# A four-layer graph network on one core: two neighbour sums of the kernel split over the column halves of TensorE

## The reference, cut to what matters

```python
# layer 2: three attention convolutions; the first has 64 inputs, 4 heads of 128 channels
h = (x @ W).reshape(n, heads, ch)
e = leaky_relu(alpha_src[src] + alpha_dst[dst], 0.2)
ex = exp(e - m[dst]);  den = segment_sum(ex, dst)
out = segment_sum(h[src] * (ex / den[dst]), dst)      # mean over heads, + bias
# layer 3: mean over neighbours
neigh_sum = segment_sum(features[src], dst)
degree = clip(segment_sum(ones, dst), 1.0)
combined = concatenate([features, neigh_sum / degree], -1) @ W + b
```

## Time and profile before

| What | Value |
|---|---|
| median of three runs | 5350.39 us |
| the profiled execution | 5350.4 us, span 5348.6 us |
| PE busy | 4615.0 us, 86% of the span |
| DVE busy | 3798.2 us, 71% |
| ACT busy | 1823.8 us, 34% |
| POOL busy | 1990.0 us, 37% |

### The profile page before, as it was taken

The page is one execution under the profiler, slowest core; times in us unless marked ns, Lnnn a source line. Parts: engine busy times, 40 slices in busy tenths (PEclk is TensorE's granted clock), DMA queues, the critical chain, the costliest instruction groups (busy, mean ns, idle before and its releaser), DMA issues.

```text
span 5348.6 us, 118073 instructions
## 1 busy us (share of the span) xinstructions
PE 4615.0 (86%) x41659; PEld 3580.5 (67%) x41660; DVE 3798.2 (71%) x5768; ACT 1823.8 (34%) x3064; POOL 1990.0 (37%) x1717
## 2 busy tenths in 40 slices
PE   6999999888886969999579999588886888888886
PEld 3998888888885555555479999564544555555554
DVE  6988888877771057777466666455114999999998
ACT  0000000000001527777337777336341333333332
POOL 3888888882002057100000000000004766666663
PEclk6999999999996879999789999789777999999998
DMA  1000000000000000000000000000001111111113
GB/s 51 6 6 5 5 5 5 5 5 1 0 0 2 0 10 10 4 2 2 20 3 4 4 4 4 17 2 11 1 3 39 37 36 36 36 36 36 36 37 25
DMA packets 203918, 74.19 MB, mean 14 GB/s; under 512 B 169275, under 2 KB 189578, under 8 KB 203658
## 3 DMA queue, kind: packets, MB, share of 16 engines
q0 software_dynamic: 52448, 31.60, 3.5%
q1 hardware_dynamic: 151338, 40.69, 3.5%
HBM read 57.25 MB, written 14.88 MB: 13 GB/s over the span
## 4 chain that ended last, share of the span: by engine, by line
PE 63%; DVE 23%; issue 8%; DVEq 3%; DMA 2%; ACT 1%; POOL 0%; SPq 0%; ACTq 0%; POOLq 0%
PE ps L1182 62%; DVE adj L1140 8%; DVE adj L1132 5%; DVE scratch L851 5%; DVEq L849 1%; DVEq L336 1%; DVE adj L1145 1%; DMA r_dram<-adj 0%; DMA hwork<-gat_out_a 0%; DMA hwork<-gat_out_b 0%; DVE hwork L849 0%; ACT scratch L555 0%; DVE adj L1125 0%; DMA scratch<-gat_out_c 0%; PE ps L1365 0%
## 5 line engine op out<-in xcount | busy, mean ns | idle before, releaser
L1182 PE MATMUL ps<-hwork,scratch 128*125 128x125 bf16 (+1 forms) x25750 | 1931.0, 236 | 99.8 <-DVE scratch L851 90.6
L1182 PEld LDWEIGHTS ps<-hwork,scratch 128*125 128x125 bf16 (+1 forms) x25750 | 1853.0, 151 | 171.6 <-DVE scratch L851 121.8
L1055 DVE SCALAR_TENSOR_TENSOR scratch<-scratch,cols,adj 125x625 f32<-125x625 f32 x1125 | 964.8, 871 | 366.9 <-ACT scratch L641 358.4
L504 POOL DMA_INDIRECT by_src<-work x782 | 1102.5, 1410 | 262.4 <-issue 224.3
L641 ACT ACTIVATE scratch<-work,cols 125x625 f32<-125x625 f32 x1125 | 1003.9, 907 | 305.4 <-PE ps L1182 242.3
L533 POOL DMA_INDIRECT adj<-r_dram,adj x832 | 808.3, 972 | 496.9 <-DMA adj<-by_src 256.1
L851 DVE TENSOR_SCALAR scratch<-hwork,edge_ids 128x3125 bf16<-128x3125 uint16 x830 | 890.3, 1073 | 0.0
L1182 PE MATMUL ps<-scratch,X 125*65 125x375 f32 (+1 forms) x3000 | 825.3, 435 | 4.8 <-DVE scratch L1055 2.7
L1182 PEld LDWEIGHTS ps<-scratch,X 125*65 125x65 f32 x3000 | 415.6, 140 | 396.1 <-issue 286.0
L519 POOL IOTA adj<- 128x125 uint16 x1 | 0.2, 246 | 1813.9 <-DVEq L1104 1813.9
L1182 PEld LDWEIGHTS ps<-adj 128*125 128x125 f16 (+3 forms) x4320 | 386.1, 158 | 419.1 <-issue 380.9
(11 more groups left out here) (253 smaller groups left out, 3075.1 us busy)
## 6 DMA issues: line engine op xcount, KB each, us to landing
adj<-r_dram,adj POOLq DMA_INDIRECT x832
adj<-q_dram SPq DMA_DIRECT2D x416, 31.2 KB
by_src<-work POOLq DMA_INDIRECT x782
by_src<-adj SPq DMA_DIRECT2D x1, 4165.0 KB
adj<-by_src SPq DMA_DIRECT2D x104, 40.0 KB, 2.0
work<-in_rec SPq DMA_DIRECT2D x46, 85.0 KB
gat_out_a<-hwork SPq DMA_DIRECT2D x5, 312.5 KB
hwork<-gat_out_a SPq DMA_DIRECT2D x1, 1562.5 KB
```

What stands on the lines that cost most here:

```text
L504: g.indirect_dma_start(by_src, bass.IndirectOffsetOnAxis(ap=pos_now[:, h, k:k + 1], axis=0), rec_in[:, h, k, :], None).then_inc(rec_sent[h ...
L1055: v.scalar_tensor_tensor(slots[:, j % SLOTS, :], slots[:, j % SLOTS, :], cols[:, 2, j, h:h + 1], adj3[:, j, ds(b * BW, BW)], ALU.add, ALU. ...
L1182: return t_.matmul(o_, l, r, start=start, stop=stop, skip_group_check=skip)
```

## The change

In the first attention layer and in the third layer's neighbour sum the stationary operand has 64 columns instead of 65. Sums of even tiles go to PSUM partitions 0 to 63, those of odd tiles to partitions 64 to 127, of the same banks. PE takes tiles in pairs: it waits for both, then issues for each bank the even tile's matmul and the odd tile's. The 25th tile of a block is alone. ACT copies 128 partitions of sums, and the projection contracts over 128 rows against weights that are loaded twice, one copy below the other, so that it adds the two halves.

In attention layer "a" the 64 columns are features 1 to 63 and the ones: `X[:, t, 1:D + 1]`. The feature that was left out is replaced by arithmetic on the weights: every row of the weights has W1's first row subtracted. The code relies on features that add up to zero over a node's 64 channels after the layer norm. The single-column matmul of the denominator now picks two rows. SP issues nine DMAs instead of four ahead of the layer, DVE waits for all nine and subtracts once over 128 x 512 in place of the clearing.

In the third layer's sum the odd tiles' casts move from ACT to DVE (12 of 25), with a semaphore of their own, `tile_by_dve`. The degrees' reciprocals of k = 0 are kept in `deg_inv` and used again, so the degree's matmul, its clamp and its reciprocal go away for k = 1. The first layer's sum (k = 0) keeps its form.

```diff
+        deg_inv = misc[:, 528:528 + NT]
+        w1_whole, w1_first = hflat[0:D, 640:1152], hflat[:, 1152:1664]
...
-                sp.dma_start(wbuf[0:fin, 0:wn], W).then_inc(s["ld"], 16)
+                sp.dma_start(w1_whole if n == "a" else wbuf[0:fin, 0:wn], W).then_inc(s["ld"], 16)
+                if n == "a":
+                    sp.dma_start(w1_first, W[0:1, :].rearrange("a c -> (a c)").partition_broadcast(128)).then_inc(s["ld"], 16)
+                    for o in (0, D):
+                        sp.dma_start(wbuf[o:o + D - 1, 0:wn], W[1:D, :]).then_inc(s["ld"], 16)
+                        sp.dma_start(wbuf[o + D - 1:o + D, 0:wn], W[0:1, :]).then_inc(s["ld"], 16)
...
+                k_agg = 2 * D if k else D + 1
...
-                    for j in range(NT):
+                    for j in range(0, NT, 1 + k):
 
                         act.wait_ge(s["tile_used"], c["tile_used"] + b * NT + j + 1)
                         a.copy(slots[:, j % SLOTS, :], adj3[:, j, ds(b * BW, BW)]).then_inc(s["tile_ready"], 1)
...
                 with dve.Fori(0, NB) as b:
+                    for j in range(1, NT, 2) if k else ():
+
+                        dve.wait_ge(s["tile_used"], c["tile_used"] + b * NT + j + 1)
+                        v.tensor_copy(slots[:, j % SLOTS, :], adj3[:, j, ds(b * BW, BW)]).then_inc(s["tile_by_dve"], 1)
                     dve.wait_ge(s["proj_ps"], c["proj_ps"] + b + 1)
...
-                        last = v.scalar_tensor_tensor(tile, proj[:, i // 3, i % 3, 0:D], inv[:, i:i + 1], tile, ALU.mult, ALU.add)
+                        last = v.scalar_tensor_tensor(tile, proj[:, i // 3, i % 3, 0:D], deg_inv[:, ds(b * BT + i, 1)], tile, ALU.mult, ALU.add)
...
+                dve.wait_ge(s["ld"], c["ld"] + 16 * (9 if n == "a" else 4))
+                w_rows = w1_whole if n == "a" else wbuf[0:fin, 0:wn]
                 if n == "a":
-                    v.memset(wbuf[D:D + 1, 0:wn], 0.0)
-
-                dve.wait_ge(s["ld"], c["ld"] + 16 * 4)
+                    v.tensor_tensor(wbuf[:, 0:wn], wbuf[:, 0:wn], w1_first, ALU.subtract)
...
+                    for j in range(0, NT, 2) if k else ():
+
+                        both = range(j, min(j + 2, NT))
+                        pe.wait_ge(s["tile_ready"], c["tile_ready"] + b * (NT // 2 + 1) + j // 2 + 1)
+                        if len(both) == 2:
+                            pe.wait_ge(s["tile_by_dve"], c["tile_by_dve"] + b * (NT // 2) + j // 2 + 1)
+                        for bank, c0, n_ in PIECES:
+                            for t in both:
+                                i = mm(ps[t % 2 * D:t % 2 * D + D, bank, 0:n_], X[:, t, 0:D], slots[:, t % SLOTS, c0:c0 + n_], t < 2, t >= NT - 2, True)
+                                if bank:
+                                    i.then_inc(s["tile_used"], 1)
...
+                            last = mm(o_[:, 0:D], aggT[:, i * T:i * T + T], wbuf[:, 0:64])
...
+                        if n == "a" and j % 2 == 0:
+
+                            both = range(j, min(j + 2, NT))
+                            pe.wait_ge(s["tile_ready"], c["tile_ready"] + q * NT + both[-1] + 1)
+                            for bank, c0, n_ in PIECES:
+                                for t in both:
+                                    i = mm(ps[t % 2 * D:t % 2 * D + D, first + bank, 0:n_], X[:, t, 1:D + 1], slots[:, t % SLOTS, c0:c0 + n_],
+                                           t < 2, t >= NT - 2, True)
+                                    if bank:
+                                        i.then_inc(s["tile_used"], 1)
```

More of the change, by code:

```diff
@@ L414, in _ @@
             sp.dma_start(wbuf[0:D, 0:64], p["L2_gnn_W"][D:2 * D, :]).then_inc(s["ld"], 16)
+            sp.dma_start(wbuf[D:2 * D, 0:64], p["L2_gnn_W"][D:2 * D, :]).then_inc(s["ld"], 16)
             sp.dma_start(wbuf[0:D, 64:128], p["L2_gnn_W"][0:D, :]).then_inc(s["ld"], 16)
@@ L579, in sage_layer @@
                     for bank, c0, n in PIECES:
-                        i = a.copy(aggT[0:D + 1, c0:c0 + n], ps[0:D + 1, bank, 0:n])
+                        i = a.copy(aggT[0:k_agg, c0:c0 + n], ps[0:k_agg, bank, 0:n])
                     i.then_inc(s["agg_out"], 1)
@@ L587, in _ @@
                 fin_ = 128 if n == "b" else D
+                k_agg = 2 * D if n == "a" else D + 1
                 act.wait_ge(s["v_ready"], c["v_ready"] + 1)
@@ L612, in copy_sums @@
                         for bank, c0, nn in PIECES:
-                            i = a.copy(aggT[0:D + 1, c0:c0 + nn], ps[0:D + 1, first + bank, 0:nn])
+                            i = a.copy(aggT[0:k_agg, c0:c0 + nn], ps[0:k_agg, first + bank, 0:nn])
                         i.then_inc(s["agg_copied"], 1)
@@ L999, in _ @@
                 v.memset(rowT[:, NB * T:(NB + 1) * T], 0.0)
-                v.tensor_scalar(small[0:D + 1, 50:51], ident[0:D + 1, D:D + 1], float(heads), None, ALU.mult)
+                if n == "a":
+                    link(v.tensor_tensor(small[:, 51:52], ident[:, D - 1:D], ident[:, 2 * D - 1:2 * D], ALU.add))
+                    v.tensor_scalar(small[:, 50:51], small[:, 51:52], float(heads), None, ALU.mult)
+                else:
+                    v.tensor_scalar(small[0:D + 1, 50:51], ident[0:D + 1, D:D + 1], float(heads), None, ALU.mult)
                 link(v.tensor_tensor(asn, a_src, by_head(top), ALU.subtract))
@@ L1265, in sage_layer @@
                 else:
-                    pe.wait_ge(s["ld"], c["ld"] + 16 * 3)
+                    pe.wait_ge(s["ld"], c["ld"] + 16 * 4)
                 for b in range(NB):
@@ L1286, in sage_layer @@
                     pe.wait_ge(s["agg_out"], c["agg_out"] + b)
-                    for j in range(NT):
+                    for j in range(NT if k == 0 else 0):
                         pe.wait_ge(s["tile_ready"], c["tile_ready"] + b * NT + j + 1)
@@ L1296, in sage_layer @@
                         o_ = ps[0:T, 6 + i // 3, (i % 3) * 129:(i % 3) * 129 + 129]
-                        mm(o_[:, 0:D], aggT[0:D, i * T:i * T + T], wbuf[0:D, 0:64])
-                        last = mm(o_[:, 128:129], aggT[0:D + 1, i * T:i * T + T], I[0:D + 1, D:D + 1])
+                        if k == 0:
+                            mm(o_[:, 0:D], aggT[0:D, i * T:i * T + T], wbuf[0:D, 0:64])
+                            last = mm(o_[:, 128:129], aggT[0:D + 1, i * T:i * T + T], I[0:D + 1, D:D + 1])
+                        else:
+                            last = mm(o_[:, 0:D], aggT[:, i * T:i * T + T], wbuf[:, 0:64])
                     last.then_inc(s["proj_ps"], 1)
@@ L1380, in project @@
                         o_ = ps[0:T, 6 + i // 3, (i % 3) * 129:(i % 3) * 129 + 129]
-                        w_ = I[0:D, 0:D] if n == "c" else wbuf[0:D + 1, h * 128:h * 128 + 128]
-                        mm(o_[:, 0:fo], aggT[0:D if n == "c" else D + 1, i * T:i * T + T], w_)
-                        last = mm(o_[:, 128:129], aggT[0:D + 1, i * T:i * T + T], small[0:D + 1, 50:51])
+                        w_ = I[0:D, 0:D] if n == "c" else wbuf[:, h * 128:h * 128 + 128]
+                        mm(o_[:, 0:fo], aggT[0:D if n == "c" else 2 * D, i * T:i * T + T], w_)
+                        last = mm(o_[:, 128:129], aggT[0:k_agg, i * T:i * T + T], small[0:k_agg, 50:51])
                     last.then_inc(s["proj_ps"], 1)
@@ L1400, in sum_tiles @@
                     for j in range(NT):
-                        pe.wait_ge(s["tile_ready"], c["tile_ready"] + q * NT + j + 1)
-                        for bank, c0, n_ in PIECES if n != "b" else ():
+                        if n == "a" and j % 2 == 0:
[7 more added lines that the diff above has]
+                                        i.then_inc(s["tile_used"], 1)
+                        if n != "a":
+                            pe.wait_ge(s["tile_ready"], c["tile_ready"] + q * NT + j + 1)
+                        for bank, c0, n_ in PIECES if n == "c" else ():
                             last = mm(ps[0:D + 1, first + bank, 0:n_], feat[:, j, :], slots[:, j % SLOTS, c0:c0 + n_], j == 0, j == NT - 1)
@@ L1408, in sum_tiles @@
                                       j == 0 and i0 == 0, j == NT - 1, True)
-                        last.then_inc(s["tile_used"], 1)
+                        if n != "a":
+                            last.then_inc(s["tile_used"], 1)
                         if has_prev and n == "b" and j == TURN_AT:
```

23 lines of the change are left out of this document (12 added, 11 removed).

## The result

The changed kernel takes 5186.89 us (median of three, 5183.94 to 5189.56) against 5350.39; the ratio of the two is 0.9696, with a 95% interval of 0.9674 to 0.9718. The forecast was 5166 us with a range of 5130 to 5260. The sign, the mechanism and the range held. The gain is 163.5 us where 184.4 had been forecast.

A forecast was written before the change was run, and what follows sets the result against it. PE was taken to set the pace in layer "a" and the third layer's sum. 5350.4 - 132 (layer "a") - 55 (third layer) + 2.5 (start of "a" and a small extra operation) = 5166 us, range 5130 to 5260.

The forecast's parts named there:

- What bounds the kernel, and the overlap: Layer "a" and third layer's sum: PE sets the pace; a pair on two column halves takes 1.15 us, between 1.05 and 1.3.
- Rival (1): Both stages: column halves do not overlap, a pair takes 2.1 us, kernel about 5353 to 5361 us; chance 0.09.
- Rival (2): Both stages: weight loads between matmuls are exposed, a pair takes 1.6 us, kernel 5246 us; chance 0.07.
- Rival (4): Only some overlap: pairs of 1.4 to 1.5 us, 25 a pass, kernel 5200 to 5215; within the forecast's 0.78.
- The pass: Layer "a": a pass falls from 30.2 to 23.6 us (21.4 to 25.2), 20 passes give -132 us (-100 to -176).
- the ring of five: Layer "a": five slots have nothing in hand, so PE's work between pairs is passed on, less 0.47 us slack.
- 137 us of idle time: Layer "a": ACT's idle time, claimed as all a faster PE could give before ACT sets the pace.
- the floor of 21.4 us a pass: Layer "a": ACT's own work, 25 x 0.81 + 0.56 + 0.61 us, the low end with everything hidden.
- The failed step: Layer "a": SP's record loads and POOL's scatter come 3 us later, first waited for in layer "b".
- The third layer: Its neighbour sum: a block falls from 33.94 to 23.3 us, with +1.8 waiting for DVE's cast; -55 us (-40 to -66).
- The clock term: Third layer's sum: a longer gap keeps the clock low for longer, +0.9 us a block (0 to 3.4).
- Ahead of layer "a": Before the first multiply: five more DMAs and a subtraction of 128 x 512 delay it by +2.3 us (0.7 to 5).

The follow-up runs named there:

- same-half run: Kernel after, with tiles 0 to 11 on the lower column half and 12 to 24 on the upper in both stages; 5359.03 us, kernel before beside it 5353.88.
- the run with places of their own: Kernel after, with a separate accumulator per block of layer "a" and the wait for the previous block's store dropped; 5169.75 us, ratio 0.9656.

## Why the prediction was right, and where its sum was off

**What bounds the kernel, and the overlap: right.** PE was the bound, and the two halves overlap. A pair takes 1.055 us in the third layer, as one tile did: nothing is lost. The forecast took 1.15 and the trace of before had only another split to go by. By "TensorE: Matmul & The Clock Gate" of the Trainium skill, Part 3, the estimate had been 1.33; the measurement is lower and decides. Rival (1) did not come about; the same-half run shows its time, though not by its terms. Rival (2) fell: no weight load comes between the matmuls of a run of pairs. Rival (4) fell with it.

**The pass: right in size, less so in its reason.** 23.25 us against 23.6. That the ring of five costs something is shown, 0.7 us a pass against a ring of six; that it has nothing at all in hand is not. One reading of the prediction was too tight: 137 us of idle time was not all that ACT could give, since its busy time itself fell by 35 us. The range went by the floor of 21.4 us a pass and was not touched by it.

**The failed step** is the sentence "SP's record loads come 3 us later; POOL's scatter then ends 3 us later, in the first quarter of layer "a" [...], and its first waiter is layer "b"". It failed twice.

- The first waiter is in layer "a". Behind the record loads in SP's queue stands block 0's store, and behind that, through `block_stored`, DVE's first head of block 1. In the kernel before the store was issued at 2124.8, was known to be complete 5.5 us later, and DVE came to that head at 2153.2: 23 us in hand. Now layer "a" comes to it 32 us earlier.
- The loads come not 3 but 12.8 us later. The first two come 2.8 us later, as forecast; the distance from load to load then grows, over the last three from 25.7 us to 27.7. Nine DMAs instead of four don't do this: in the same-half run, which has the nine and a slow layer "a", the last load goes out at 2113.85 us, earlier than in the kernel before; in the kernel after and the ten other runs with the halves side by side it goes out at 2124.4 to 2130.6. So the scatter takes longer where the other engines run layer "a" faster; why is not shown. With loads only 3 us late the wait would be an estimated 5 us (2119.8 + 0.9 to the store + 5.3 to its end, less 2121.3) in place of 14.5.

In all this cost 17.1 us by the run with places of their own. The queue, the semaphore and the times of the last load and of DVE were in the trace of before; that the scatter slows was not.

**The second omission** is the turn of DVE's loop, 4.4 us three times: 12.3 us by the run with the loop written out. It could not be read from the trace of before, where the same turn shows 0.30 us.

**The clock** is the third: in the run with DVE's loop written out, seven passes stand 11.2 us over 23.25 in all, with low stretches in them. Against the forecast's 600.4 - 132 = 468.4 us that makes 464.2 + 17.1 + 12.3 + 11.2 = 504.8, and 505.8 was measured. That it comes so close is in part luck, as the passes with a low clock differ from run to run (11.2 us over in seven passes in one run, 8.3 in five in the next).

**The third layer: mechanism right, terms mis-sized.** The block is 20.34 us and the forecast 23.3. Tiles at the full clock are 12 x 1.055 + 1.05 = 13.7 instead of 14.9, the wait for DVE 2.51 instead of 1.8. The clock term had the wrong sign: the forecast added 0.9 us for a longer low stretch, and kept the old one of the earlier trace rows. After, the whole low stretch costs 1.9 us, and the projection runs at the full clock in 1.31 us (windows at 1.00), where it fell into the low stretch before. The sum was 15 us too small for the gain, and hid a part of the other error.

**Ahead of layer "a"**: nine issues from 1904.85 to 1908.47 us, the subtraction at 1912.51, the first multiply of weights at 1913.12 against 1909.66; less 1.0 us by which the stage had already started later, +2.5, the forecast's +2.3. The last stretch, layers "b" and "c", changed by under 4 us, as was said.

## What to carry to other kernels

Two sums with 64 output rows each ran side by side on separate column halves in the time of one, in either order tried inside the pair; what does not split was cheaper in one piece between them than in several. When the bound of a stage is halved, list every wait that had slack under it (stores in a shared queue, first operations of a block) with its time from the trace, not from the stage's new pace: here two such waits took 32 us (17.1, and 14.5 by the traces) of what the change could give, and each was a few lines to remove. An engine that only runs alongside (POOL here) need not keep its old pace when the others speed up. Compare the same place of both traces before a stall is put down to lost slack: the loop turn, 12 us, was not there before. A short wait ahead of a matmul run can cost twice, once by itself and once by the clock after it.

## What the runs showed of the hardware that was not expected

- Column halves of the array overlap fully for f32: 1.055 us for a pair of tiles against 1.05 for one, with both weight loads on the same 125 rows and no gap for either.
- A change between two column halves and the whole array costs 0.1 us (0.14 before the chunk, 0.09 after it; in the kernel before, without the change, no more than 0.03 for both).
- The turn of one and the same VectorE loop of 264 recorded instructions took 0.30 us of idle time in the kernel before and 4.3 to 4.7 in the kernel after and in the same-half run; code written out for 16 passes shows none. What makes the difference is open.
- POOL's scatter slows when the other engines run denser: the last three record loads of layer "a" go out 27.7 us apart instead of 25.7, and the last two of the same-half run 24.0 apart.
- TensorE fell to the lower level of its clock after 2.5 us without a matmul between stretches of dense work (0.57 on average over the next 4 us), and did not after 0.5 us. After 1.1 to 1.2 us in layer "a" it fell in some passes and not in others.
